# Turning experts' rows by transposing DMAs in a cross-attention and mixture-of-experts kernel

## The reference

```python
x = x + xattn(layernorm(x), ctx)            # W_qkv 128x3072, W_out 1024x128
xt = layernorm(x)                           # 4096 tokens, 128 channels
logits = xt @ Wg.T + bg                     # 16 experts
top_vals, top_idx = top_k(logits, 2)
cw = softmax(top_vals) placed at top_idx
gu = einsum('th,ehf->tef', xt, Wgu) + bgu   # 256 wide: gate and up interleaved
gate, up = minimum(gu[..., ::2], 7), clip(gu[..., 1::2], -7, 7)
gated = (up + 1) * gate * sigmoid(1.702 * gate)
out_e = einsum('tef,efh->teh', gated, Wd) + bd
x = x + einsum('teh,te->th', out_e, cw)
```

## Time and profile before

| | |
|---|---|
| median of 3 runs | 601.31 us (600.66 to 601.98) |
| span of the profiled execution | 636.7 us |
| its own time beyond the span | not on record |
| mean granted TensorE clock in it | 0.949 |
| TensorE busy in the span | 85% |
| VectorE, ScalarE, GpSimd busy | 82%, 76%, 71% |

### The profile page before, as it was taken

How to read it: one execution, slowest core, us unless ns; L and a number is a source line. 1 busy time by engine, 2 the same in 40 slices (tenths; PEclk the granted TensorE clock), 3 DMA queues, 4 the chain that set the end, 5 groups by cost and what they waited for, 6 DMA issues and landing times.

```text
span 636.7 us, 20049 instructions
## 1 busy us (share of the span) xinstructions
PE 542.6 (85%) x6760; PEld 457.3 (72%) x6760; DVE 519.7 (82%) x1482; ACT 484.4 (76%) x1366; POOL 450.0 (71%) x555
## 2 busy tenths in 40 slices
PE   2899999999999999999999999977778687778700
PEld 1578898988999889889898899876435565556500
DVE  5879999999999999999999999988756456465516
ACT  1899999999999999999999999978425445455410
POOL 8996585988989889889898898753533455545530
PEclk9999999999999999999999999999789879898755
DMA  9772383174062947228337407550122332221139
GB/s 258 222 274 53 59 287 68 46 261 124 19 185 72 308 132 248 60 57 302 81 55 267 125 12 221 175 119 3 28 62 70 82 82 66 69 69 56 33 115 302
DMA packets 69701, 81.63 MB, mean 128 GB/s; under 512 B 8116, under 2 KB 47564, under 8 KB 69604
## 3 DMA queue, kind: packets, MB, share of 16 engines
q1 hardware_dynamic: 56244, 67.60, 36.8%
q0 software_dynamic: 4352, 8.47, 4.0%
q10 hardware_dynamic: 9008, 4.30, 2.5%
HBM read 18.82 MB, written 46.31 MB: 102 GB/s over the span
## 4 chain that ended last, share of the span: by engine, by line
PE 66%; DVE 9%; issue 7%; ACT 7%; DMA 3%; ACTq 2%; another core or an unknown queue 2%; POOL 2%; SPq 0%; POOLq 0%
PE bank L1258 15%; PE bank L1259 15%; PE bank L1260 15%; PE bank L1378 8%; PE bank L1430 5%; PE bank L1466 3%; DMA ctx_sb<-results 2%; ACT probs L564 2%; PE bank L1497 1%; PE bank L1524 1%; ACTq L462 1%; POOL results L833 1%; DVE pT L1071 1%; ACT pT L576 1%
## 5 line engine op out<-in xcount | busy, mean ns | idle before, releaser
L564 ACT ACTIVATE probs<-bank,nbias 128x128 f32<-128x128 f32 x512 | 146.4, 369 | 4.2
L833 POOL DMA_INDIRECT results<-z,stage x72 | 71.0, 986 | 73.3 <-ACT z L618 53.0
L1071 DVE TENSOR_TENSOR pT<-bank,pT 128x512 f16<-128x512 f32 x128 | 87.6, 684 | 10.9 <-ACT pT L576 7.8
L1050 DVE TENSOR_REDUCE qmax<-bank 128x4 f32<-128x512 f32 x128 | 87.1, 680 | 2.0 <-remote 1.4
L1260 PE MATMUL bank<-keys,q_pad 128*128 128x128 f16 x480 | 86.7, 219 | 0.3 <-issue 0.3
L1259 PE MATMUL bank<-keys,q_pad 128*128 128x128 f16 x480 | 86.6, 219 | 0.0
L1258 PE MATMUL bank<-keys,q_pad 128*128 128x128 f16 x480 | 86.6, 219 | 0.0
L576 ACT ACTIVATE pT<-bank 128x512 f16<-128x512 f32 x128 | 78.2, 611 | 7.2 <-PE bank L1378 4.6
L1378 PE MATMUL bank<-ident,probs 128*128 128x128 f32 x512 | 78.4, 276 | 5.5 <-DVE pT L1071 2.9
L770 POOL DMA_INDIRECT places<-payload,slots x64 | 65.3, 1020 | 16.3 <-issue 11.8
L1258 PE MATMUL bank<-xT,w_qkv 128*128 128x256 f16 x256 | 69.9, 273 | 1.1 <-DVE xT L879 0.8
(11 more groups left out here) (261 smaller groups left out, 2015.5 us busy)
## 6 DMA issues: line engine op xcount, KB each, us to landing
places<-z SPq DMA_DIRECT2D x8, 4160.0 KB
q_pad<-q_nat SPq DMA_DIRECT2D x120, 128.0 KB, 2.4
stage<-places SPq DMA_DIRECT2D x64, 65.0 KB
ctx_sb<-results SPq DMA_DIRECT2D x14, 256.0 KB, 5.0
ctx_sb<-in_ctx_dram ACTq DMA_DIRECT2D x4, 512.0 KB, 10.6
stage<-in_L_ffn_Wgu_dram SPq DMA_DIRECT2D x1, 2048.0 KB, 9.5
out_dram<-x_sb ACTq DMA_DIRECT2D x7, 256.0 KB, 5.5
stage<-in_L_xattn_W_qkv_dram SPq DMA_DIRECT2D x3, 512.0 KB, 6.6
```

What stands on the lines that cost most here:

```text
L564: last = nc.scalar.activation(probs[:, b, k, :], score_bank[b][:, k * P:(k + 1) * P], ACT.Exp, bias=nbias[:, b, k:k + 1], scale=exp_scale)
L833: nc.gpsimd.indirect_dma_start(out=results, out_offset=bass.IndirectOffsetOnAxis(ap=to, axis=0), in_=z[:, (q - 5) % NZ, t, :], in_offset=None,
L1050: nc.vector.tensor_reduce(qmax[:, r % 2, :], score_bank[r % 2][:, :].rearrange("p (h k) -> p h k", h=4), AX.X, ALU.max).then_inc(s["qmax_o ...
L1071: nc.vector.tensor_tensor(pT[:, r % 2, LO, :], pt_bank[:, :], pT[:, r % 2, HI, :], ALU.subtract).then_inc(s["pt_lo"], 1)
```

## The change

The rows of a pair no longer arrive as they lie in `places`, to be turned on TensorE. SP issues for each block a transposing DMA of the 256 float16 columns into `turned` (in `stage`), so that they arrive with channels on partitions, high and low halves apart, and a second, plain DMA with the two last words of every row into `tags`. Each pair so has four DMAs on SP, and TensorE waits for 64 instead of 32 on the buffer's semaphore. The four (two) transposes, their two banks, the copy bT and its semaphores are gone.

The banks that this frees make gate/up four banks deep, and gate, up, sigmoid, hidden (now `inner`) and hT have four buffers (`DEPTH`), which lie in tiles that attention no longer uses. The lags are longer: in step q TensorE computes gate/up of pair q, the down product of pair q-5, and transposes hidden of pair q-3, in this order. ScalarE's order is hT of pair q-4, the sigmoid of q-1, z of q-6. VectorE's low half is that of q-4, and GpSimd sends q-6.

A shared pair is no longer set apart between zeros. TensorE computes the second expert's product on all 128 rows, and then the first expert's product on rows 0 to 63, which overwrites that half (`portions`). The zeroing at the end of attention and its semaphore are gone.

```diff
-        bT = sb("bT", [P, 2, 2, 2, P], F16)
-        gate = sb("gate", [P, 2, 2, P])
-        up = sb("up", [P, 2, 2, P])
+        tags = sb("tags", [P, NBUF, 2, 2])
+        turned = stage[:, 0:NBUF * 256].bitcast(F16).rearrange("p (b t h n) -> p b t h n", b=NBUF, t=2, h=2)
+        wide = q_nat[:, :, :, :, :, :].rearrange("p a b h i n -> p (a b h i n)").bitcast(F32).rearrange(
+            "p (w k t n) -> p w k t n", w=4, k=DEPTH, t=2)
+        gate, up, sigs, inner = (wide[:, w] for w in range(4))
-        hT = sb("hT", [P, 2, 2, 256], F16)
+        hT = keys[:, :, :, :, :].rearrange("p a h b n -> p (a h b n)")[:, 0:DEPTH * 512].rearrange("p (k h n) -> p k h n", k=DEPTH, h=2)
...
-        rows_in = stage[:, 0:NBUF * 2 * ROW].rearrange("p (b t w) -> p b t w", b=NBUF, t=2)
-        rows16 = rows_in[:, :, :, 0:P].bitcast(F16)
-
-        t_bank = [banks[0][:, :].bitcast(F16), banks[1][:, :].bitcast(F16)]
-        gu_bank, ht_bank, d_bank, table_bank = banks[2:4], banks[4:6], banks[6:8], banks[7]
+        gu_bank, table_bank = banks[0:4], banks[7]
+        ht_bank, d_bank = banks[4:6], banks[6:8]
...
@@ -434,14 +432,14 @@
                     if q == 0:
                         for par in range(2):
                             sp.wait_ge(scattered[par], 64 * (PAIRS // 2))
-                    if q == NBUF - 1:
-                        sp.wait_ge(s["gu_lo"], 8)
                     wait_sent(sp, q - NBUF)
                     n = P if tiles(q) == 2 else HALF
                     for t, at in enumerate((both % 2048, both // 2048)):
                         place = nc.s_assert_within(at, 0, NE * ROOM // HALF, skip_runtime_bounds_check_because="the table holds no other") * HALF
-                        to = rows_in[:, u, t, :] if tiles(q) == 2 else rows_in[t * HALF:(t + 1) * HALF, u, 0, :]
-                        sp.dma_start(to, places[bass.ds(place, n), :]).then_inc(block_in[u], 16)
+                        to = turned[:, u, t, :, :] if tiles(q) == 2 else turned[:, u, 0, :, own(t)]
+                        sp.dma_start_transpose(to, places[bass.ds(place, n), 0:P].bitcast(F16)).then_inc(block_in[u], 16)
+                        to = tags[:, u, t, :] if tiles(q) == 2 else tags[own(t), u, 0, :]
+                        sp.dma_start(to, places[bass.ds(place, n), P:ROW]).then_inc(block_in[u], 16)
...
-                    if (p, r) == (PAIRS, 7):
-                        act.wait_ge(s["score_mm"], ALLQ)
-                        for k in range(2):
...
@@ -610,36 +600,23 @@
             nc.scalar.activation(spare[:, :], zeros[:, 0:1], ACT.Sigmoid)
 
             def expert_steps(q, u, i):
-                if block_live(q, 5):
-                    wait(act, "d_mm", q - 4)
-                    wait_sent(act, q - 5 - NZ)
-                    n = tiles(q - 5)
+                if block_live(q, 4):
+                    k, n = (q - 4) % DEPTH, tiles(q - 4) * P
+                    wait(act, "ht_mm", q - 3)
+                    wait(act, "d_mm", q - 7)
+                    nc.scalar.activation(hT[:, k, HI, 0:n], ht_bank[k % 2][:, 0:n], ACT.Copy).then_inc(s["ht_hi"], 1)
+                if block_live(q, 1):
+                    k, n = (q - 1) % DEPTH, tiles(q - 1)
+                    wait(act, "gate_ok", q)
+                    wait(act, "glu_ok", q - 4)
+                    nc.scalar.activation(sigs[:, k, 0:n], gate[:, k, 0:n], ACT.Sigmoid, scale=ALPHA).then_inc(s["sig_ok"], 1)
+                if block_live(q, 6):
+                    k, n = (q - 6) % DEPTH, tiles(q - 6)
+                    wait(act, "d_mm", q - 5)
+                    wait_sent(act, q - 6 - NZ)
                     for t in range(n):
-                        nc.scalar.activation(z[:, (q - 5) % NZ, t, :], d_bank[(u + 1) % 2][:, t * P:(t + 1) * P], ACT.Copy,
-                                             scale=rows_in[:, (q - 5) % NBUF, t, P:P + 1]).then_inc(s["z_ok"], 2 // n)
...
-                if block_live(q, 1):
-                    wait(act, "gate_ok", q)
-                    wait(act, "glu_ok", q - 2)
-                    n = tiles(q - 1)
-                    nc.scalar.activation(sig[:, (u + 1) % 2, 0:n], gate[:, (u + 1) % 2, 0:n], ACT.Sigmoid, scale=ALPHA).then_inc(s["sig_ok"], 1)
+                        nc.scalar.activation(z[:, (q - 6) % NZ, t, :], d_bank[k % 2][:, t * P:(t + 1) * P], ACT.Copy,
+                                             scale=tags[:, (q - 6) % NBUF, t, 0:1]).then_inc(s["z_ok"], 2 // n)
...
+                if block_live(q, 6):
+                    n = tiles(q - 6)
+                    for t in range(n):
+                        wait(pool, "z_ok", 2 * (q - 6) + (t + 1) * (2 // n))
+                        to = tags[:, (q - 6) % NBUF, t, 1:2].bitcast(U32)
...
@@ -1213,31 +1191,26 @@
 
             def expert_steps(q, u, i):
                 if block_live(q, 2):
+                    k, n = (q - 2) % DEPTH, tiles(q - 2)
+                    nc.vector.tensor_tensor(glu[:, 0:n, :], gate[:, k, 0:n], sigs[:, k, 0:n], ALU.mult).then_inc(s["glu_ok"], 1)
                     wait(dve, "glu_ok", q - 1)
-                    wait(dve, "ht_mm", q - 3)
-                    nc.vector.scalar_tensor_tensor(out=hidden[:, u % 2, 0:n], in0=up[:, u % 2, 0:n], scalar=1.0 - LIMIT,
+                    wait(dve, "ht_mm", q - 5)
+                    nc.vector.scalar_tensor_tensor(out=inner[:, k, 0:n], in0=up[:, k, 0:n], scalar=1.0 - LIMIT,
...
+                    k, n = (q - 1) % DEPTH, tiles(q - 1)
                     wait(dve, "gu_mm", q)
-                    wait(dve, "h_ok", q - 2)
+                    wait(dve, "h_ok", q - 4)
+                    bank = gu_bank[k][:, :].rearrange("p (t c f) -> p t c f", t=2, c=2)
...
+                        nc.vector.tensor_scalar(to[:, k, 0:n], bank[:, 0:n, c, :], scale_from[:, 5:6], most,
+                                                ALU.mult, ALU.min).then_inc(s[done], 1)
+                if block_live(q, 4):
+                    k, n = (q - 4) % DEPTH, tiles(q - 4) * P
+                    wait(dve, "ht_hi", q - 3)
+                    nc.vector.tensor_tensor(hT[:, k, LO, 0:n], ht_bank[k % 2][:, 0:n], hT[:, k, HI, 0:n], ALU.subtract).then_inc(s["ht_lo"], 1)
...
+            def plus_bias(dst, a_hi, a_lo, b_hi, b_lo, bias):
+                nc.tensor.matmul(dst, ones16[:, 0:a_hi.shape[-1]], bias, start=True, stop=False)
+                return three(dst, a_hi, a_lo, b_hi, b_lo, start=False)
...
-            def load_experts(v, i):
+            def load_experts(v):
 
-                    six = pe.value_load(expert_groups[0:1, i * (NBUF // 3) + g:i * (NBUF // 3) + g + 1], min_val=0, max_val=NE ** 6 - 1)
+                    known.pop(g - 3, None)
+                    six = pe.value_load(expert_groups[0:1, g:g + 1], min_val=0, max_val=NE ** 6 - 1)
...
+            def portions(v):
+
+                first, second = experts_of(v)
+                return ((0, P, first), (1, P, second)) if tiles(v) == 2 else ((0, P, second), (0, HALF, first))
+
                 if block_live(q, 0):
-                    pe.wait_ge(block_in[u], i * 32 + 32)
-                    wait(pe, "t_ok", q - 1)
...
+                    k = q % DEPTH
+                    load_experts(q)
+                    pe.wait_ge(block_in[u], (i + 1) * 64)
+                    wait(pe, "up_ok", q - 3)
+                    if q < DEPTH:
+                        fill(gu_bank[k], 2)
+                    for t, rows, e in portions(q):
+                        last = plus_bias(gu_bank[k][0:rows, t * 256:(t + 1) * 256], turned[:, u, t, HI, 0:rows], turned[:, u, t, LO, 0:rows],
+                                         w_gu[:, HI, e, :], w_gu[:, LO, e, :], bias_gu[:, e, :])
                     last.then_inc(s["gu_mm"], 1)
+                if block_live(q, 5):
+                    k = (q - 5) % DEPTH
+                    wait(pe, "ht_lo", q - 4)
+                    wait(pe, "z_ok", 2 * (q - 6))
+                    for t, rows, e in portions(q - 5):
+                        at = slice(t * P, t * P + rows)
+                        last = plus_bias(d_bank[k % 2][0:rows, t * P:(t + 1) * P], hT[:, k, HI, at], hT[:, k, LO, at],
+                                         w_d[:, HI, e, :], w_d[:, LO, e, :], bias_d[:, e, :])
+                    last.then_inc(s["d_mm"], 1)
                 if block_live(q, 3):
+                    k = (q - 3) % DEPTH
                     wait(pe, "h_ok", q - 2)
                     wait(pe, "ht_lo", q - 4)
                     for t in range(tiles(q - 3)):
-                        last = nc.tensor.transpose(ht_bank[(u + 1) % 2][:, t * P:(t + 1) * P], hidden[:, (u + 1) % 2, t, :], ident[:, :])
+                        last = nc.tensor.transpose(ht_bank[k % 2][:, t * P:(t + 1) * P], inner[:, k, t, :], ident[:, :])
                     last.then_inc(s["ht_mm"], 1)
```

(40 more changed lines are left out.)

72 lines of the change are left out of this document (3 added, 69 removed).

## The result

The changed kernel takes 699.59 us (median of 4, 697.08 to 700.8), the kernel before in the same comparison 601.64 us (4 runs, 600.66 to 602.39): ratio 1.1624, 95% interval 1.1603 to 1.1644, 98 us slower. The profiled execution of the changed kernel has an own time of 700.1 us and a span of 698.4.

What follows compares the result with a forecast made beforehand. GpSimd's 72 sends were taken to bound the kernel before, ending at 575.6 us; SP's 114 us of issuing, landing, last product and ten sends put the changed kernel's last at 601.2, so +25.6 on 601.3: 627 us, range 589 to 670.

Steps and rivals of the forecast that it cites:

- The bound: Experts' stage: GpSimd's 72 sends bound the kernel before, 2.57 us a whole pair; SP's issuing bounds the changed one, 2.85.
- GpSimd's floor: Experts' stage: 72 sends at 1.285 us from start to start cannot end sooner than 91.2 us after the first.
- The price of a transposing DMA on SP: SP's queue: taken as a plain load's 0.333 us; far end GpSimd's 0.98 us, 4.15 us a pair, 679 us in all.
- The second load per block: SP's queue: four DMAs a pair instead of two, 2.85 us instead of 1.71, 114 us for forty pairs; +25.6 us.
- The removals on TensorE and ScalarE: Experts' stage: transposes and ScalarE's copy bT, 22.3 us, go; worth nothing beside GpSimd's sends.
- The spells as the cost of recording: Recorded experts' stage: stretches where all engines slow down, taken as caused by recording and absent from ordinary runs.
- 36.7 and 35.4 us: Sends' lateness in the recorded stage, and the recorded execution's excess over a run; near equality taken as showing recording's cost.
- Rival 1: Experts' stage: spells are real in runs, SP's stream 12 buffers ahead rides over them; 11 us less, 590 us; chance 0.15.
- Rival 2: SP's queue: below 2.3 us a pair without recording, GpSimd stays the bound, only the start moves; 603 us; chance 0.13.
- Rival 3: DMA engines: turned rows go in small pieces; 659 us at 64 bytes, about 702 by the skill's 1309 ns; chance 0.20.
- Longer lags, four banks: Experts' stage: z moves from lag 5 to 6; four gate/up banks stay empty with SP as bound and give nothing.
- TensorE's clock: TensorE's matmuls: a slower clock, 421 ns among the 280, could add when TensorE waits for every block; no size given.

Runs made afterwards that it cites:

- g0_before_again: Kernel before, unchanged, recorded again on a chip without spells: 602.77 us beside 603.91, span 601.0.
- g3_longer_sends: Kernel before with a 128 x 256 float32 memset on GpSimd ahead of each of 72 sends, chip without spells: 612.22 us, ratio 1.0145.
- g1_plain_rows: Changed kernel with plain loads replacing transposing ones, tags still apart, rows unturned, chip without spells: 629.90 us beside 603.91 of the kernel before, ratio 1.0449.
- g2_one_dma_per_block: Changed kernel with one plain load of whole rows per block, rows unturned, chip without spells: 598.8 us, ratio 0.991 to the kernel before.
- e0_before_again: Kernel before, unchanged, recorded again on the chip with spells: 641.06 us beside 640.55, span 639.3.
- e1_plain_rows: Changed kernel with plain loads replacing transposing ones, tags still apart, rows unturned, chip with spells: 653.6 us beside 640.55 of the kernel before, ratio 1.0194.
- h1_pe_turns_a_step_ahead: Changed kernel with one plain load per block, TensorE turning rows a step ahead, ScalarE copying, two gate/up banks: 604.84 us, ratio 1.0031 to the kernel before.
- h3_tags_from_scalar_queue: Changed kernel with the tags' loads issued from ScalarE's queue, four pairs ahead: 645.38 us, ratio 1.0709 to the kernel before.
- after: Profiled execution of the changed kernel itself, nothing further edited: own time 700.1 us, span 698.4.
- h2_transposes_of_half_the_columns: Changed kernel with each transposing DMA taking 128 instead of 256 columns, TensorE reading the high half twice: 696.29 us beside 602.65 of the kernel before.

## Why the prediction was right and wrong

- **The bound.** Right for the changed kernel: SP's issue time, GpSimd's sends no longer a limit, DMA engines far from full, no long wait on `z_sent`, ten sends in a row at the end. For the kernel before it was not quite right: TensorE sets the pace there, 6.5 us above GpSimd's floor (`g0_before_again`, `g3_longer_sends`).
- **The price of a transposing DMA on SP: the step that failed.** The prediction put it at the plain 0.333 us, "since it is the same queue and the same kind of issue", with GpSimd's 0.98 as the far end. It is 1.195, outside both. With that number its own sum would have been 627 + 80 x 0.862 = 696 us, against 699.6. That it comes so near is in part luck, because two shortfalls cancel. From SP's first load to the last send the sum so mended has 130.4 + 69 = 199.4 us and the trace 210.4 (464.2 to 674.6); for the kernel before it has 104.8 (470.8 to 575.6) and the trace 111.3 (465.4 to 576.7). Even its far end, 679, was short. An upper bound taken from another instruction on another engine was no bound.
- **The second load per block.** Right in kind: forecast +25.6 us at the plain price, measured +26.0 (`g1_plain_rows`). The match to 0.4 us is luck. SP took 3.1 us a pair on average where the sum had 2.85, so that 139.1 us lie between first load and last send (464.8 to 603.9) instead of 130.4; and the kernel before was longer than reckoned by nearly as much, as said above. Behind a transposing load the tags' instruction is 0.43 instead of 0.333 us, 80 x 0.1 = 8 us that the sum didn't have; the move that a transposing load lacks gives 6 back.
- **The removals on TensorE and ScalarE.** Nearly right: counted at nothing, measured 5 us together with lags and banks (`g2_one_dma_per_block`). The reason given, GpSimd as the bound, holds only behind the first 6.5 us: so much TensorE could gain before GpSimd's floor stopped it.
- **The spells as the cost of recording.** Wrong (`e0_before_again`). The use made of it came out nearly right all the same: a chip on which the kernel takes 603 us shows no spells. But that GpSimd's last send, reckoned at 575.6, is at 576.7 there is luck: its first is 5.4 us earlier than in the record (479.0 against 484.4), and from first to last they take 97.7 us, not 91.2. The nearness of 36.7 and 35.4 us has another reason, as far as the times of the chips tell: the profile came from a chip with spells and the 601.31 from one without. Rival 1 had it right that spells are in the runs, of the chip that shows them; with SP at 4.6 us a pair no stream ahead of the spells was left to gain by it. Even at the plain price the change does not gain there: 653.6 us beside 640.55 (`e1_plain_rows`), where the rival had 11 us less.
- **Rival 2** needed SP below 2.3 us a pair; SP took 4.6. Its remark that the longer lags move the start is borne out by 481.3 against 479.0 (`g2_one_dma_per_block`), 2.3 us where it had 2.1; with TensorE still turning it was 6 (`h1_pe_turns_a_step_ahead`).
- **Rival 3** had the wrong mechanism, and a time of the right size only by a figure from outside the trace: the load queue takes 14.7% of the DMA engines, its packets are 226 bytes and not 64 (`h3_tags_from_scalar_queue`), and it is SP that is full. The Trainium skill's page VectorE: DVE Perf Modes, section The three transpose paths, gives 1309 ns for one 128x128 transpose by DMA; from it the prediction had an estimate of 5.2 us a pair and 702 us. Two transposing instructions measure 2.4 us of SP's time here, each turning two such tiles, and the kernel takes 699.6. The totals are close by luck: a block of two tiles and half of it cost SP nearly the same (1.195 and 1.12 us), and nearly half of SP's 4.6 us a pair is tags, arithmetic and gaps. The page Advanced Engine Details and Errata, section X-Bar Transpose (TRN2), says that such transfers run as fast as ordinary ones. For the time on the DMA engines the trace nearly agrees, 81 us of one engine per MB against 69. For the rest it does not: 2.4 us from instruction to landing against 1.9 for plain rows (`g1_plain_rows`), and 1.195 us of SP against 0.333.
- **Longer lags, four banks.** Forecast to give nothing with SP as the bound; no run took them away alone, but the chain of the stage holds only SP. Without the DMAs and with TensorE turning, the kernel with them, its two gate/up banks kept, starts its sends 6 us later and saves 3.3 (`h1_pe_turns_a_step_ahead`).
- **TensorE's clock**, named as a thing that could add: 0.68 of 2.4 GHz on average in the stage, and the first matmul of a block (L1437) is 350 ns in the mean where the earlier trace rows has 280. In the middle it lies beside SP's time. At the end the last product's eight matmuls take 2.0 us instead of 0.9, about 1.1 of the 2.7 us by which the way to the first of the ten sends was longer than forecast; the other 1.6 is ScalarE's queue, where the sum left out that the sigmoid stands behind L607.

## What to carry to other kernels

When work moves from a computing engine to a DMA, count its instructions on the queue that issues them, each with address arithmetic and gaps, and set them against the pace of the stage: here 2.57 us a pair were to be had and SP needed 4.6. If the trace doesn't show the kind of DMA that is to be added, its issue price is unknown, and a neighbour's price is no bound on it; measure that one instruction first. Splitting one load in two to make half of it transposable costs a full issue, however small the second half: 8 bytes a row cost SP as much as 512 (0.333 us each in `g1_plain_rows`). And where two engines are nearly full, as TensorE and GpSimd were here within 6.5 us, taking work off the one is worth only the distance to the other.

## What the runs showed of the hardware

- A transposing DMA with a register address holds SP for 1.195 us (1.16 at the least, 2.2 at the most, `after`), with 128 columns 1.12 (`h2_transposes_of_half_the_columns`), with 64 rows no less; a plain one 0.333. It lands 2.4 us after its start, a plain one after 1.9 (`g1_plain_rows`).
- A small plain load behind it takes SP 0.43 us instead of 0.333. Issued from ScalarE's queue instead it takes 0.346 (`h3_tags_from_scalar_queue`).
- GpSimd's indirect DMAs follow each other every 1.285 us at best, 0.98 busy and 0.30 between (`g0_before_again`).
- The same kernel takes 602.7 to 605.3 us on three chips and 640.6 on another. In a record of the slow kind all engines, SP's queue included, slow down in the same spells, and the recorded execution takes what the others on its chip take (641.06 and 640.55 us). The cause is open.
